# Identity matmuls on TensorE at the start of eight stage runs of a two-layer decoder

## The reference

```python
x = x + linear_attention(layernorm(x))             # L0_attn, random features, causal
x = x + cross_attention(layernorm(x), ctx_512)     # L0_xattn, 16 heads of 64
x = x + local_transformer(layernorm(x))            # L0_ffn: two layers, each
#         h = shift_token(x); x = x + local_attention(h @ wqkv) @ wo   (8 heads of 64, window 64)
#         h = layernorm(shift_token(x)); x = x + (a * gelu(g)) @ w2 + b2
x = x + mamba_both_ways(layernorm(x))              # L1_attn
x = x + context_attention(layernorm(x), ctx_512)   # L1_xattn, 16 heads of 8
x = x + experts(layernorm(x))                      # L1_ffn: 16 experts, top 2
```

## Time and profile before

| | us |
|---|---|
| median of three runs | 4106.53 (4106.15 to 4109.89) |
| the profiled execution | 4106.24 |
| its span, first to last instruction | 4104.5 |
| TensorE busy | 3875.4 (94%) |
| VectorE busy | 3014.3 (73%) |
| ScalarE busy | 2846.5 (69%) |
| GpSimd busy | 1809.5 (44%) |
| mean granted TensorE clock | 0.987 |

### The profile page before, as it was taken

One profiled execution on the slowest core, in us unless ns is written; L12 is line 12 of the kernel. 1 busy time (PEld: TensorE's weight loads), 2 busy tenths in 40 slices (PEclk: granted clock), 3 DMA queues, 4 the chain that ended last, 5 costly groups with the idle time before them and its releaser, 6 DMA issues. The chain is left out here.

```text
span 4104.5 us, 107091 instructions
## 1 busy us (share of the span) xinstructions
PE 3875.4 (94%) x34248; PEld 3012.2 (73%) x34248; DVE 3014.3 (73%) x7587; ACT 2846.5 (69%) x6420; POOL 1809.5 (44%) x1728
## 2 busy tenths in 40 slices
PE   8999899999979999898999989999999989998999
PEld 5677678888746666685666677888888867776777
DVE  7888665555569999658999955777777767776665
ACT  6666555555569999757999965777777767775333
POOL 3333222222268888526777753333333321112443
PEclk9999999999999999999999999999999999999999
DMA  0000100000000000100000010000000000000000
GB/s 18 9 10 9 48 8 6 6 6 6 22 28 8 8 8 8 27 17 10 8 8 8 14 29 27 1 0 0 0 0 0 0 3 3 3 3 6 12 12 13
DMA packets 109259, 42.48 MB, mean 10 GB/s; under 512 B 91232, under 2 KB 107872, under 8 KB 108512
## 3 DMA queue, kind: packets, MB, share of 16 engines
q1 hardware_dynamic: 109152, 41.10, 3.9%
HBM read 20.16 MB, written 4.19 MB: 6 GB/s over the span
## 5 line engine op out<-in xcount | busy, mean ns | idle before, releaser
L1138 POOL TENSOR_TENSOR l_rc<-l_rc,l_rs 128x1024 f32<-128x1024 f32 x128 | 303.7, 2373 | 201.5 <-DVE l_rs L1330 199.8
L1205 ACT ACTIVATE l_prob<-l_prob,l_mx 128x128 f32<-128x128 f32 x1024 | 311.9, 389 | 0.0
L1816 POOL TENSOR_TENSOR mb_steps<-w_upto,mb_dta 128x1024 f32<-128x1024 f32 x64 | 121.5, 1898 | 354.4 <-DVE mb_dta L2073 354.4
L707 POOL TENSOR_TENSOR ca_prob<-ca_prob,ca_sm 128x1232 f32<-128x1232 f32 x64 | 144.0, 2250 | 299.3 <-DVE ca_sm L873 299.3
L1230 PE MATMUL l_qk_ps<-w_local,l_hT 128*128 128x512 f32 x512 | 248.9, 609 | 12.5 <-DVE l_rs L1330 9.3
L1132 POOL TENSOR_TENSOR l_prob<-l_prob,l_sm 128x1024 f32<-128x1024 f32 x128 | 243.0, 1898 | 16.9 <-DVE l_sm L1316 16.9
L1115 POOL TENSOR_TENSOR l_rc<-l_rc,l_ss 128x1024 f32<-128x1024 f32 x128 | 243.6, 1903 | 12.5 <-POOL l_rc L1138 4.5
L1973 PE MATMUL mb_x_ps<-w_wx,mb_xT 128*128 128x256 f32 x1024 | 236.9, 384 | 0.0
L1325 DVE TENSOR_REDUCE l_ss<-l_sq 128x16 f32<-128x1024 f32 x128 | 156.1, 1219 | 77.7 <-ACT l_sq L1169 77.1
L2532 POOL TENSOR_TENSOR mo_hid<-mo_hid,mo_gate 128x1024 f32<-128x1024 f32 x64 | 121.8, 1903 | 199.8 <-DVE mo_hid L2678 199.8
L1973 PEld LDWEIGHTS mb_x_ps<-w_wx,mb_xT 128*128 128x128 f32 x1024 | 190.0, 191 | 23.2
(11 more groups left out here) (354 smaller groups left out, 12156.9 us busy)
## 6 DMA issues: line engine op xcount, KB each, us to landing
la_xin<-in_x SPq DMA_DIRECT2D x64, 64.0 KB
l_h<-lt_y SPq DMA_DIRECT2D x128, 32.0 KB
lt_quad<-lt_y SPq DMA_DIRECT2D x32, 128.0 KB
out_x<-k_x SPq DMA_DIRECT2D x64, 64.0 KB, 1.5
l_h<-lt_y SPq DMA_DIRECT2D x128, 31.8 KB
lt_quad<-lt_y SPq DMA_DIRECT2D x32, 127.0 KB
ca_ctxT<-in_ctx_T SPq DMA_DIRECT2D x128, 19.2 KB
wr_state<-in_p_state SPq DMA_DIRECT2D x1, 2438.5 KB, 11.9
```

Source lines behind the costliest of these rows:

```text
L1138: gp.tensor_tensor(wide(rc[l][:]), wide(rc[l][:]), wide(rs[l][:]), ALU.add).then_inc(*pool_sum.did("rot"))
L1205: ex = sc.activation(p[:, a, j], p[:, a, j], ACT.Exp, bias=mx[l][:, a, j:j + 1])
```

## The change

A function `spin` issues `count` matmuls of the identity with itself into a PSUM bank that the stage's first real results don't use until later. It is called on TensorE's program behind the opening waits of the stages, with 8 spins in cross attention, 30 in local attention (both layers), 19 in the gated MLP (both layers), 15 in mamba, 16 in context attention and 8 in the experts; and in local attention with 16 more ahead of the waits of the first sequence's Q and K product. Linear attention has none.

```diff
+def spin(te, g, bank, count):
+
+    for _ in range(count):
+        te.matmul(bank[:, 0:T], g.ident[:], g.ident[:], start=True, stop=True)
 ...
                 te.wait_ge(zeroed, NZERO)
+                spin(te, g, y_ps, 8)
 ...
                 te.wait_ge(g.fetched, g.NLOCAL)
                 te.wait_ge(zeroed, NZERO)
+                spin(te, g, v_ps, 30)
 ...
                     b = at(QKV)
                     if b:
+                        if b.trip is None and b.base == 0:
+                            spin(te, g, v_ps, 16)
                         te.wait_ge(*act_hT.at("hT", b))
                         te.wait_ge(*vec_rot.at("sin1", b, ago=1))
 ...
                 te.wait_ge(zeroed, NZERO)
                 te.wait_ge(g.fetched, g.NLOCAL)
+                spin(te, g, o_ps, 19)
 ...
                 te.wait_ge(zeroed, 4)
+                spin(te, g, out_ps, 15)
 ...
                 te.wait_ge(zeroed, NZERO + 4)
                 te.wait_ge(g.fetched, g.NLAST)
+                spin(te, g, out_ps, 16)
 ...
                 te.wait_ge(g.fetched, g.NLAST)
+                spin(te, g, y_ps, 8)
```

## The result

The changed kernel takes 4123.02 us (median of six runs, 4118.89 to 4124.31) against 4107.07 for the kernel before (six runs, 4106.15 to 4109.89): ratio 1.0035, interval 1.0025 to 1.0046, 16 us slower. The forecast was 4110.9 with a range that ended at 4118. In the experiments one run in ten of the kernel e3 took 16967.87 us and is left out of its median (4115.53; 4115.88 with it).

What follows compares the result with a forecast made beforehand. TensorE was taken to bound the middle of stages, with starts passed on one to one. Local attention +9.3 and the other starts -4.9 made +4.4 us: 4110.6 on the profiled execution, 4110.9 as median, range 4103 to 4118.

Steps and rivals of the forecast that it cites:

- What bounds the kernel, and that starts are passed on one to one: Mid-stage TensorE is busy 426.04 of 440 us; behind barriers, what a stage's start gains or loses moves the end equally.
- The price of a spin: Each spin on TensorE costs 0.22 us at the full clock, 0.43 at the low one.
- How soon spinning lifts the clock: At stage starts, 3.4 to 5.4 us of spinning lifts the clock from 0.50 to 1.00.
- The 16 ahead of the first product, and the 1.9 back: Local attention: 16 spins delay the first Q and K product; running warm, it gives 1.9 us back.
- Local attention in sum: Both local-attention starts: +3.4 us in layer 0, +5.9 in layer 1, together +9.3.
- The other starts, -4.9: Cross attention -1.1, gated MLP -0.7 per layer, mamba -1.2, context attention 0, experts -1.2 us.
- Context attention's bound of +3: Context attention: up to 3 us slower if the sparse work that follows lets the clock fall again.
- The sum: Whole kernel: 9.3 - 4.9 = +4.4 us, median 4110.9, +0.11%, likeliest verdict no change.
- (1): All starts: spins don't lift the clock and cost 0.43 us each once it has fallen; +41 us, 4148; chance 0.04.
- (3): Stage starts: the clock doesn't fall, since spinning begins before it would; 4098.9, -0.19%; chance 0.08.
- (2): Local-attention starts lose +9.3 us and gains elsewhere don't reach the end; 4115.8, slower by 0.23%; chance 0.19.
- What would show it: Timeline signs: layer 0's 30 spins last about 8 us, second Q and K product cold, cold stretches 60 to 80 us.

Runs made afterwards that it cites:

- e3: The kernel before plus only the 30 spins ahead of local attention's first transposition, both layers: 4115.53 us, +7.0.
- e11: The kernel before plus only 60 spins ahead of local attention's first transposition, both layers: 4128.43 us (two runs), +19.3.
- e9: The kernel before plus, in local attention only, 13 spins at the start, 16 ahead of the second Q and K product, 10 ahead of the first score part: 4105.52 us, -3.6.
- e4: The kernel before plus only the 16 spins ahead of local attention's first Q and K product, both layers: 4114.63 us, +6.1.
- e1: The kernel before plus only the change's spins in local attention (30, then 16, both layers): 4123.30 us, +14.8.
- e2: The kernel before plus the change's spins in all the other stages, none in local attention: 4107.02 us, -1.5.
- e12: e9 plus the 19 spins of the gated MLP and the 8 of the experts: 4106.86 us, -3.7 against the kernel before.
- e10: The kernel before plus only the 15 spins of mamba and the 16 of context attention: 4108.99 us, -0.1.
- e7: The kernel before plus only 60 transpositions of the identity ahead of local attention's first transposition, both layers: 4111.78 us, +4.2.
- e5: The kernel before plus only 16 spins ahead of local attention's second Q and K product, both layers: 4110.21 us, +2.6.
- e8: The kernel before plus only 13 (layer 0) and 9 (layer 1) spins ahead of local attention's first transposition: 4108.20 us, +0.6.

## Why the prediction was wrong, point by point

- **What bounds the kernel, and that starts are passed on one to one:** right, and e11 shows it most plainly: 8.4 us late at the third step, 8.5 at the stage's end.
- **The price of a spin:** right. In the changed kernel the product behind 16 warm spins starts 3.57 us after the first of them (1158.87 - 1155.30), 0.22 us each; 13 cold ones fill 5.54 us, 0.43 each.
- **How soon spinning lifts the clock, the step that failed first:** I took 3.4 us in layer 0 and 5.4 in layer 1. It was 5.54 (1145.77 to 1151.31) and 6.05 (1851.82 to 1857.87). The transposition was 3.7 late instead of 2.4, and 5.6 instead of 5.0. The range of 3.4 to 5.4 was read from three cases, and the first of them, 525.45 to 528.86, is the length of a cold stretch and not a time from the start of work: TensorE had been busy for 1.90 of the 3.65 us before it, too. e11's layer 1 had 2.9 (1854.96 to 1857.82), e9's layer 1 3.4 (1847.18 to 1850.57), its layer 0 6.0 (1148.27 to 1154.25), context attention in the changed kernel 6.2 (3346.68 to 3352.91): 2.9 to 6.2 is what the runs show for spins that begin at the low clock and last long enough.
- **The 16 ahead of the first product, and the 1.9 back:** right in size. The forecast had 2.9 for the 16 in layer 0 and 2.8 in layer 1, behind an early transposition; in the changed kernel the product is 6.6 - 3.7 = 2.9 and 8.4 - 5.6 = 2.8 later than the transposition, and 1.9 comes back in each. Alone (e4) they make the product 4.4 and 5.0 late, since some then run cold, and 2.5 and 3.0 of that are left behind the 1.9.
- **Local attention in sum:** forecast +3.4 and +5.9, in the profile +5.4 and +7.3. Of the 3.3 us between them 1.3 and 0.6 are the slower rise. Most of the rest is a drop of the clock about 35 us into each stage (1178.62 and 1885.17) that costs 1.2 and 1.1, where my sum ended with the second Q and K product and set all behind it at nothing; some 0.4 and 0.3 come back on the way. By medians (e1, +14.8) the term is 5.5 above the forecast's +9.3. e1's own profile has 5.7 + 7.4 = 13.1 in the two stages; the other 1.7 is no more than what stages with the same code move between two executions, and stays open.
- **The other starts, -4.9:** didn't arrive; e2 has -1.5, with 0 as good a reading. The experts did what was said: 1.0 shorter (forecast 1.2), and 0.9 in e2 and e12, where kernels without their spins show 0.2 at most. In the gated MLP the first gelu is unmoved, 13.28 us from its stage's start (1717.83 - 1704.55, before 1710.00 - 1696.73 = 13.27), but the gain behind it (forecast 0.7 for each layer) is not there: the second stage is unchanged, and the 0.5 by which the first is shorter is no gain of the spins, since all eleven profiles without spins there, that of the same kernel once more among them, show 0.3 to 0.5 too. Cross attention (forecast -1.1) is 1.4 longer, but its stage is 3.9 longer in e1, which has its code as before, so no size is to be read from one profile. Mamba's 15 spins took 6.19 us and let its transposition go 3.6 us late, not 0.9. The forecast had all 15 at the full clock (2534.12 + 15 x 0.22 = 2537.4), and here the clock was low for the first 5.44 us of them:

```profile
2548.75 6.19 PE L228 MATMUL mb_out_ps<-k_ident 128*128 128x128 f32 x30 [3.58 <-DVE mb_seg_ps L2021]
2554.78 0.27 PE L2013 MATMUL mb_out_ps<-k_ident,mb_xn 128*128 128x128 f32 x1
```

  It came out 0.9 longer where 1.2 shorter was forecast; with the same spins it is 0.3 and 0.2 shorter in e2 and e10. Context attention's bound of +3, set for the case that the clock falls again behind the spins, was reached: +3.6.
- **The sum:** forecast +4.4, measured +16.0. The local term was +14.8 instead of +9.3, the others -1.5 instead of -4.9. The two make 13.3; the 2.7 to 16.0 is less than the width of either interval, and stays open.
- **Rivals:** (1) is excluded by e7. (3) held in one layer of e7. (2), the local starts lose and the gains don't reach the end, is what happened, but as worked out it gave 4115.8 and carried 0.19; the time lay 7 us beyond it. What it lacked is, as far as the runs show, what the forecast lacked: the slow rise, and drops of the clock further down the filling.
- **What would show it:** the warm first product, the cold second and the unmoved gelu came as said. The 30 spins of layer 0 took 9.58 us, not 8, the context transposition was 4.4 us late, not 3, and the low stretches fell to 85.33, not to 60 to 80: three readings of the one mis-sized step. The closing sentence, that a warm second product would take 2 us per layer off, is wrong: e5 made it warm, and GpSimd's 4.2 us behind the same release took its place.

## What to carry to other kernels

Spins ahead of a stage's first operand are paid in full for every one that outlasts the wait, so count them at the low clock's price (0.43 us here, against a wait of 4 to 6 us) and for the slowest rise seen, not for the mean. A warm product is worth something only if it is the last thing its successor waits for: look beside it for the engine that the same semaphore released, and follow the timeline to the end of the filling, since in most layers here a later drop of the clock took back part of the gain, whether the waits between were covered or not. The time spent at the low clock is no measure of such a change; here it fell by 24 us while the kernel lost 16, and the best version, with spins only in waits that could hold them, gained 3.6, with an interval from 1 to 8.

## What the runs showed of the hardware that was not expected

- Transpositions of an f32 identity lift the granted clock as products do, 5.61 us after they began against 5.54.
- From the first spin at the low clock to its rise took 2.9 (e11, layer 1) to 6.2 us (context attention in the changed kernel), and 6.0 and 3.4 in the two layers of one execution (e9). In layer 1 of e7 the clock hadn't fallen at all, and in that of e8 it fell only 2.7 us behind the last spin.
- The same kernel spent 109.20 us at the low clock in one execution and 133.10 in another, with 3.9 us between the spans. Differences of 2 to 4 us between single profiles are therefore no evidence; the verdicts above rest on the medians of many runs, and the readings of the table on shifts that repeat.
